# Loading the direct half of an adjacency matrix from two DMA queues instead of one, in a graph layer with a mixture of experts

## What is computed

```
z    = layernorm(x)
mask = (adj > 0)                                    # 4096 x 4096
agg  = mask @ z / max(rowsum(mask), 1)
x1   = x + relu(concat(z @ W_self + b_self, agg @ W_nb + b_nb) @ W_comb + b_comb)
xf   = layernorm(x1)
out  = x1 + sum over the top 2 of 8 experts of weight * (gelu(xf @ W1[e] + b1[e]) @ W2[e] + b2[e])
```

## Time and profile before

| | |
|---|---|
| median of three executions | 525.25 us |
| lowest, highest | 524.35, 525.72 us |
| span of the profiled execution | 521.0 us |
| busy: TensorE, its weight loads | 444.2 us (85%), 380.2 us (73%) |
| busy: VectorE, ScalarE, GpSimd | 370.7 (71%), 257.6 (49%), 305.2 us (59%) |
| SP's queue | 68.29 MB, 47.2% of 16 DMA engines' span |
| GpSimd's queue | 50.49 MB, 32.4% |
| ScalarE's queue | 2.88 MB, 1.9% |

### The profile page before, as it was taken

One profiled execution on the slowest core, in us unless ns is written; L12 is line 12 of the kernel. 1 busy time (PEld: TensorE's weight loads), 2 busy tenths in 40 slices (PEclk: granted clock), 3 DMA queues, 4 the chain that ended last, 5 costly groups with the idle time before them and its releaser, 6 DMA issues.

```text
span 521.0 us, 12708 instructions
## 1 busy us (share of the span) xinstructions
PE 444.2 (85%) x4162; PEld 380.2 (73%) x4162; DVE 370.7 (71%) x1056; ACT 257.6 (49%) x403; POOL 305.2 (59%) x346
## 2 busy tenths in 40 slices
PE   4599989999999999989799899745999999997720
PEld 3388878888888888768688688633887778876610
DVE  2889744858758888679587798662677777679982
ACT  2558660543634354344354342330677777776630
POOL 2679778244355766756567563676255556555570
PEclk9789999999999999989999899965799999999975
DMA  8999898599999999999999931964555555588665
GB/s 247 267 264 270 239 243 221 147 278 258 256 272 277 298 306 307 299 297 276 301 282 307 291 132 62 275 230 153 166 164 164 164 161 153 149 325 335 195 211 161
DMA packets 49167, 122.47 MB, mean 235 GB/s; under 512 B 11081, under 2 KB 20173, under 8 KB 48080
## 3 DMA queue, kind: packets, MB, share of 16 engines
q1 hardware_dynamic: 31632, 68.29, 47.2%
q0 software_dynamic: 16080, 50.49, 32.4%
q10 hardware_dynamic: 1392, 2.88, 1.9%
HBM read 96.52 MB, written 26.93 MB: 237 GB/s over the span
## 4 chain that ended last, share of the span: by engine, by line
PE 27%; DVE 21%; DMA 19%; issue 12%; ACT 6%; SPq 6%; POOL 5%; another core or an unknown queue 2%; DVEq 1%; ACTq 0%; POOLq 0%
DMA wst<-in_L_ffn_W_dram 11%; PE bank L1326 7%; PE bank L1346 7%; PE bank L1227 6%; SPq L440 5%; POOL stage L563 3%; DMA x_sb<-in_x_dram 2%; DMA stage<-in_adj_dram 2%; PE bank L1218 2%; PE bank L1219 2%; DMA stage<-in_adj_dram,gidx 2%; PE bank L1313 2%; DVE stage L1112 2%; DVE mask L820 2%
## 5 line engine op out<-in xcount | busy, mean ns | idle before, releaser
L1218 PE MATMUL bank<-z_flat,maskT 128*128 128x257 f16 x1024 | 231.6, 277 | 0.7 <-issue 0.4
L1219 PE MATMUL bank<-z_lo,maskT 128*128 128x256 f16 x1024 | 231.5, 276 | 0.0
L642 POOL DMA_INDIRECT pair_out<-rows,enum x78 | 79.6, 1021 | 66.9 <-DVE gate L1125 29.7
L563 POOL DMA_INDIRECT stage<-in_adj_dram,gidx x64 | 76.0, 1188 | 64.3 <-ACT mask L667 52.0
L1218 PEld LDWEIGHTS bank<-z_flat,maskT 128*128 128x128 fp8e4 x1024 | 101.4, 99 | 14.2 <-issue 0.5
L1219 PEld LDWEIGHTS bank<-z_lo,maskT 128*128 128x128 fp8e4 x1024 | 101.4, 99 | 13.0 <-issue 0.3
L574 POOL DMA_INDIRECT dispatched<-rows,slot x64 | 65.9, 1030 | 39.5 <-issue 20.2
L710 ACT ACTIVATE xh<-x_sb,nb,rs 128x256 f32<-128x256 f32 x32 | 19.2, 600 | 139.6 <-POOL nb L631 139.6
L667 ACT ACTIVATE mask<-stage,m 128x2048 fp8e4<-128x2048 int32 x32 | 64.0, 2001 | 15.2 <-DVE maskT L827 7.5
L1346 PE MATMUL bank<-w,stage 128*128 x468 | 60.7, 281 | 8.2 <-DVE stage L1112 4.3
L1326 PE MATMUL bank<-stage,w 128*128 128x256 f16 x468 | 61.4, 284 | 6.2 <-DVE stage L1098 4.4
(11 more groups left out here) (175 smaller groups left out, 586.0 us busy)
## 6 DMA issues: line engine op xcount, KB each, us to landing
stage<-in_adj_dram SPq DMA_DIRECT2D x256, 128.0 KB
stage<-dispatched SPq DMA_DIRECT2D x39, 260.0 KB
wst<-in_L_ffn_W_dram SPq DMA_DIRECT2D x16, 256.0 KB
z_lo<-pair_out SPq DMA_DIRECT2D x4, 1024.0 KB
dispatched<-pad SPq DMA_DIRECT2D x15, 260.0 KB
out_dram<-x_sb SPq DMA_DIRECT2D x28, 128.0 KB
maskT<-pair_out SPq DMA_DIRECT2D x3, 1024.0 KB, 8.5
x_sb<-in_x_dram ACTq DMA_DIRECT2D x6, 256.0 KB, 8.5
```

What stands on the lines that cost most here:

```text
L563: gp.indirect_dma_start(out=stage[:, s, b - 2, :], out_offset=None, in_=adj_q[:, :], in_offset=bass.IndirectOffsetOnAxis(ap=gidx[:, 0:1], ...
L642: gp.indirect_dma_start(out=yp_dram[:, :], out_offset=bass.IndirectOffsetOnAxis(ap=enum[:, a, s:s + 1], axis=0), in_=ysb[:, a, s, :], in_o ...
L1218: mm(acc[u % 2][:, 0:D + 1], a, z_hi[:, i, :], start=(i == 0), stop=False)
L1219: last = mm(acc[u % 2][:, 0:D], a, z_lo[:, i, :], start=False, stop=(i == NT - 1))
```

## The change

SP now loads only the quadrants g = 0 and 1 of each direct half (partitions 0 to 63), four transfers of 128 KB a tile. ScalarE gets a `load_adj` of its own for g = 2 and 3 (partitions 64 to 127), four transfers a tile on its own queue. It waits for VectorE's mask as SP's does. ScalarE calls it for tile 0 between the two normalisations at the start, for tile 1 among the first casts, for tiles 2 to 7 right behind its own mask in the first stage, and for tiles 8 to 31 at the head of `main_step`.

```diff
@@ SP, load_adj(t)
                 for b in range(2):
-                    for g in (0, 2, 1, 3):
+                    for g in (0, 1):
                         sp.dma_start(stage[Q * g:Q * g + Q, s, b, :], adj_v[t // B, t % B, g, :, b, :]).then_inc(s_adj[s], 16)
@@ ScalarE
+            def load_adj(t):
+                s = 2 * (t % 2)
+                if t >= 2:
+                    act.wait_ge(s_mD, t - 1)
+                for b in range(2):
+                    for g in (2, 3):
+                        act.dma_start(stage[Q * g:Q * g + Q, s, b, :], adj_v[t // B, t % B, g, :, b, :]).then_inc(s_adj[s], 16)
...
-            for k in range(OWN // B):
-                normalise(k)
-            for i in range(AHEAD - 1):
+            normalise(0)
+            load_adj(0)
+            normalise(1)
+            for i in range(AHEAD - 2):
                 zt_hi(i)
+            load_adj(1)
+            zt_hi(AHEAD - 2)
...
                 if i in MASKS:
                     t = MASKS.index(i)
                     masks(t, t, t)
+                    load_adj(t + 2)

             def main_step(t, u, known):
+                if HELD < known < NT - MADE - 1:
+                    load_adj(t + MADE + 1)
                 if live(known, NORM):
```

## The result

The changed kernel took 530.81 us (median of four executions, 527.01 to 537.3), the kernel before 524.8 us beside it. The ratio is 1.0139, with a 95% interval of 1.0083 to 1.0196: slower, by 7.3 us by the ratio and by 6.0 us between the medians. Run again in two other groups, on two different chips, it gave 1.0134 (1.0082 to 1.0186) and 1.0216 (1.0151 to 1.0280).

What follows compares the result with a forecast made beforehand. It took TensorE to bound the first stage, and TensorE and the DMA engines to be near the limit in the neighbour stage. Terms 0 + 9 + 0 - 2 = +7 us gave 532 us, range 521 to 543.

Steps and rivals of the forecast that it cites:

- Tiles 2 to 7: First stage: ScalarE's loads wait for VectorE's masks and delay its copies, costing 9 us, between ends of 4.8 and 17.8.
- the 17.8 us I had: First stage: ScalarE held up by six loads, 6.6 us waiting for VectorE's masks plus 11.2 us of issue.
- They hold the engine up: ScalarE's four transfers a tile block the engine while issued, 1.87 us, judged from the table load behind ten transfers.
- the load does not hold ScalarE up: Rival: loads issue beside running work, so the first stage pays only waits; about 525 us, within the draw's 0.10.
- Tiles 0 and 1: Start of the kernel: the loads go into ScalarE's idle time, cost 0, ends 0 and 1.87 us each.
- Tiles 8 to 31: Neighbour stage: 24 loads fit the gap before `xh`, 0.6 us left, cost 0; about 12 us if that cover goes.
- The queues: Neighbour stage: weights land sooner but the DMA engines are full, so -2 us, between ends of -15 and +5.
- It stands behind a full megabyte: Neighbour stage: an expert-weight load takes 14.89 us to land because a megabyte of adjacency precedes it in SP's queue.
- a sign of being wrong: Prediction wrong if neighbour products start before 82 us, or what follows them, 442.7 us, changes by more than 6 us.
- The starving gather: Rival: in the neighbour stage the gather gets a third of the DMA rate, costing 14 us; 548 us, chance 0.12.
- The faster case: Rival: three queues bring weights early, neighbour stage gains 12 us, first stage pays 5; 518 us, chance 0.15.

Runs made afterwards that it cites:

- the split by halves: SP loads quadrants 0 and 1, ScalarE 2 and 3, only from tile 8 on, against the kernel before: 0.9886, and 0.9938 on another chip.
- the wrong split: Kernel in which ScalarE loads from tile 8 on, but SP takes quadrants 0 and 2, ScalarE 1 and 3: ratio 1.0286 against the kernel before.

## Why the prediction was right

**Sign and size** were right: +7 us forecast for the median, +6 measured, and the ratio's interval is +4 to +10 us. But two terms of the sum were both too small in size, and their errors cancelled. That the total came out so near is luck.

**Tiles 2 to 7, "I take 9 us".** The mechanism was right in each step: the wait for VectorE's mask, the transfers, the late copy, TensorE's stop in front of pair 6. The size was 12.7 us (in the last group 12.9: 66.8 against the 53.9 of the kernel that loads from tile 8 on). TensorE's stops grew by 9.2 us, which is the 9 of the sum. What it left out is the clock. I had noted the half clock for the neighbour stage but not for this one, and TensorE's stops brought it here as well: 4.33 us in place of 2.78 and 3.59 in place of 1.99, 3.2 us together. The six loads also held ScalarE up a little longer than the 17.8 us I had: 20.5 us, of which 8.8 for VectorE's masks (3.1, not 2.45, at the second) and 11.7 for the issue (2.60, not 1.87, at the second). TensorE stopped in front of pairs 6, 13 and 15, as I had said, but in front of pair 9 and not of pair 11.

**"They hold the engine up"** is true of what stands behind the transfers: in every load shown the next copy starts after their end. It need not delay what stands ahead. The rival *the load does not hold ScalarE up*, because it is issued beside running work, came true for the first load of the kernel with the load one pair later, and the row I set against it, the table load behind ten transfers, could not exclude it: no work stood ahead of those. How much the holding up costs was set by whether the copies that TensorE needs stand ahead.

**Tiles 0 and 1, cost 0.** Right as far as the profiles tell: the first stage's products begin between 24.8 and 26.4 us in the six with these loads, between 24.3 and 26.4 in the eight without.

**Tiles 8 to 31, cost 0.** Right in the main: in the step shown the load ends 0.6 us before `xh`, as the row had it. A few transfers took longer (2.90 us at 181.96 us, in place of 1.79), and the neighbour stage became shorter all the same.

**The queues, "I take -2 us, because rows 2 show the engines full and the bytes don't change".** This is the step that failed. The term was about -7 us in the changed kernel (256.3 to 249.2). The other profiles by halves, without the one that sends the weights first, have 247.0 to 252.5 us, and those with the order 0, 2, 1, 3 on one queue 253.4 to 256.3, so -5 us is the better figure. A DMA share of 1.04 is not a rate: nearly equal shares (1.00 to 1.04) moved 246 to 279 GB/s from 120 to 160 us. "It stands behind a full megabyte", the reason I gave for the late weights, was not the cause either, as the experiment with the weights on ScalarE's queue shows. The rule of the Trainium skill that I weighed, in DMA: Bandwidth & Descriptors, section "Issuing engines are not separate DMA queues", would have had 0 here. It holds for the weights moved alone (ratio 1.0027) and not for the split by halves (0.9886 and 0.9938). Where they differ the measurement decides.

**The signs.** I had named as a sign of being wrong that what comes behind the first neighbour product changes by more than 6 us. It was 442.4 us against 442.7, but only because 6.8 of the 7.1 us gained in the neighbour stage were lost again in the expert stage, which the change doesn't touch. So this sign passed by chance.

**The rivals.** The starving gather did not come: ScalarE's waits for it, 3.9 us in the kernel before, are gone from the list, where I expected more. The faster case named the right waits (10.8 and 9.9 us, now 3.5 and 5.0) with the wrong cause: moving the weights to another queue did nothing, sharing the adjacency by halves did.

**Left open.** The quadrant g chooses the partitions, and also which quarter of each row is read, so these runs don't tell whether the memory's side or the chip's own buffer sets the rate. A kernel that keeps the partitions and exchanges the quarters was not tried. Nor do the runs tell why the second queue adds to the right grouping; that the gather gets a smaller part of the engines beside two other queues is one reason that they leave open. Why one load of weights still took 17.61 us in the changed kernel (216.16 on the chain of waits) is open too.

## What to carry to other kernels

A DMA issue on a computing engine holds up what stands behind it, with its wait. Put it behind the work that the bottleneck engine needs next, not right behind the thing it waits for: here the same 24 transfers cost 12.7 us, or 0.7 to 3.2 one pair later, though ScalarE still stood idle for 14.0 us behind them. A full DMA share says little about the rate: try the order and grouping of transfers before counting queues, since the order alone was worth 2.5% and the wrong split 3.5%. Where an edit has parts in two stages, run the parts apart; here one half was the faster kernel.

## What was not expected of the hardware

- Order on one queue: the same eight transfers of 128 KB, as quadrants 0, 1, 2, 3 in place of 0, 2, 1, 3, moved 246 in place of 263 GB/s from 120 to 160 us at the same DMA share of 1.04.
- ScalarE's queue takes transfers while its engine still computes, if their wait is met: two went out at 36.02 us beside a copy that ran from 35.95 to 36.65, and the next copy started at 37.80, after the fourth had gone out at 37.74.
- Expert weights on a queue by themselves (2 x 256 KB) still left VectorE waiting 7.6 us, and two of the loads took 18.3 and 19.7 us to land.
